# The offset convolution in 32 by 32 tiles with four bank exchanges, in place of two 64-wide column tiles

## The chip, the cores and the metric

The kernel runs on one core of a Trainium2 chip. The metric is the device time of one execution in microseconds (us); lower is better. TensorE is PE in the rows, its weight loads PEld; VectorE is DVE, ScalarE ACT, GpSimd POOL, SyncE SP.

## The reference, cut to what matters

Eight images of 32 channels and 192 by 192 pixels pass two layers, each with a group norm and a residual. The first layer has a 3 by 3 convolution that gives two offsets for every channel and pixel (`w_off`), bilinear sampling at these offsets, and a second 3 by 3 convolution of the samples. The change lies in the first of these convolutions.

```python
x = x + _L0_conv_ref(_gn(x), w_off, b_off, w_dcn, b_dcn)
x = x + _L1_conv_ref(_gn(x), w1, b1, w2, b2)
...
off = (jax.nn.sigmoid(conv2d(x, w_off, b_off, OFFSET * D, D)) - 0.5) * (2.0 * OFFSET)
...
v00 = planes[nidx, j0, i0]
...
sampled = v00 * (1 - wy) * (1 - wx) + v01 * (1 - wy) * wx + v10 * wy * (1 - wx) + v11 * wy * wx
return conv2d(sampled.reshape(b, c, h, w), w_dcn, b_dcn, P, D)
```

The second layer averages its normed input, makes a 3 by 3 kernel for each channel from the averages, and convolves each channel with it (depthwise).

## The kernel before, in words

The 128 partitions hold 32 channels of four neighbouring image rows (quarter g has row g of a group). A chunk is four such groups, 16 image rows; an image has 12 chunks, the program 96. All data are fp32, and TensorE runs an fp32 matmul in two passes, each with its own weight load, which stand as two records.

Each chunk has three views in `xv`: MID, its rows as they are, and ABOVE and BELOW, the same moved by one image row up and down. `xv` has three slots, filled by SyncE (`x_load`), with GpSimd setting the pads (`set_pads`).

The offset convolution is `offsets(n, i)`, at L402 through `conv`. For each offset i (across, down) and each half h of the chunk it makes six matmuls with 128 input rows, 64 output columns and 384 moving columns: the tap kx = 0, 1, 2, for two column tiles, the lower half of the partitions from ABOVE and the upper from BELOW. The weights `wos` are banded: a block of 128 by 64 holds the three vertical taps where they belong and zeros elsewhere. The result lies in the four PSUM banks of `z` (i, h). `off_mm` rises by one after i = 0 and by one after i = 1, and ScalarE's `offset(n, i)` (L614, Tanh of z into `du` or `dv`, signal `z_read`) waits for it; then come the signs `mu`, `mv` (L621), a mirrored row at an image's edge (L643) and the sizes (L628). VectorE selects neighbours by the signs (L818, L825, L826) and blends them (L835 to L851) into `sr`, shifted by SyncE into `sh`.

The program order on TensorE is written out by hand. In step i it does `depthwise(c, 0)`, `offsets(i, 0)`, `offsets(i, 1)`, `depthwise(c, 1)`, `deform(d, 0)`, `deform(d, 1)`, with c = i - 19 and d = i - 3. `deform` is the second convolution (`dc`, L442, and `fe` at an image's edge, L451), in four 32-wide column tiles of 128 rows. `depthwise` is the second layer's (`dw`, L475), in two 64-wide ones; `dw` is a single bank, and each depthwise half waits on `o_done` until ScalarE's `finish` (L649) has read the half before. ScalarE does, in step i: evacuation of dc (L669), sums for the next image (L655, L658), `finish(c, 0)`, Tanh, sign and size for i = 0 and for i = 1, `finish(c, 1)`, a square (L679), and `sides(i + 1)` (L635). The steps of an image's norm are small matmuls into `sm` and small GpSimd operations; `x_norm` in step 10 and `x_weights` in step 11 of an image make mean and scaled weights of the next (`wos` at L908).

Of the kernel before, what the change touches and what calls it, by code (L numbers as in the profile page):

```python
# [28 lines left out]
STILES = 8  # L29
SW = HW // G // STILES  # L30
# [36 lines left out]
def x_dmas(n):  # L67
    return 3 + (n % CHUNKS in (0, CHUNKS - 1))
# [37 lines left out]

def small_order():
# [13 lines left out]
def block_kernel(nc, x, planes, w_off, b_off, w_dcn, b_dcn, w1, b1, w2, b2, consts, xr, w_edge, pivots, w1x, out):  # L121
    with ExitStack() as ctx:
# [6 lines left out]
        xv = [sb(f"xv{s}", [P, 3, NB, WP]) for s in range(XS)]  # L129
# [14 lines left out]
        wo = sb("wo", [P, 2, 3, 2 * C])  # L144
        wo_sum = sb("wo_sum", [P, 2, 2 * C])
        wd_sum = sb("wd_sum", [P, Q, C])
        mr = [sb(f"mr{s}", [P, 1]) for s in range(2)]
        wos = [sb(f"wos{s}", [P, 2, 3, 2 * C]) for s in range(2)]
# [76 lines left out]
        off_mm = sem("off_mm")  # L225
        z_read = sem("z_read")
# [56 lines left out]
        def _(sp):  # L283
            def x_load(n):
# [4 lines left out]
                for view in range(3):  # L289
# [4 lines left out]
                    if j == CHUNKS - 1 and view == BELOW:  # L294
# [4 lines left out]
                                 blocks_of(b, line + P * k0, k1 - k0)).then_inc(done, 16)  # L299

# [94 lines left out]
        def _(pe):  # L395
# [3 lines left out]
            def conv(acc, weights, whole, moved):  # L399
                for kx in range(3):  # L400
                    for m, view in zip(halves, (whole, moved)):
                        last = nc.tensor.matmul(acc[m], weights[:, kx, :], view[:, :, kx:kx + W],  # L402
                                                start=kx == 0, stop=kx == 2)
                return last

            def offsets(n, i):
                b, j = divmod(n, CHUNKS)
                v = xv[n % XS]
                if i == 0:
                    pe.wait_ge(x_in[n % XS], ring(n, XS, x_dmas))  # L410
                    pe.wait_ge(pads, pads_set(n))
                    if j == 0:
                        pe.wait_ge(wo_ok, b + 1)
                wait(pe, z_read, 2 * (n - 1) + i + 1)
                for h in range(2):
                    k = slice(HALF * h, HALF * h + HALF)
                    last = conv(z[:, i, h, 0:HALF * W], wos[b % 2][:, i], v[:, ABOVE, k, :], v[:, BELOW, k, :])
                last.then_inc(off_mm, 1)
# [77 lines left out]
            def x_biases(b):  # L496
# [3 lines left out]
                for i in range(2):  # L500
                    for g, m in enumerate(quarters):
                        half = slice(C * (g % 2), C * (g % 2) + C)
                        nc.tensor.matmul(sm[m, C_OB + i:C_OB + i + 1], wo_sum[:, i, half], mean, start=True, stop=True)
# [50 lines left out]
            for i in range(TOTAL):  # L554
# [6 lines left out]
                offsets(i, 0)  # L561
                offsets(i, 1)
# [247 lines left out]
        def _(dve):  # L810
# [57 lines left out]
            dve.wait_ge(x_row, 1)  # L868
            for view in (ABOVE, BELOW):
# [287 lines left out]
```

## Time and profile before

| | before |
|---|---|
| median of 3 runs | 1492.13 us (1490.91 to 1494.03) |
| profiled execution, own time | 1493.54 us |
| its span, first to last instruction | 1491.7 us |
| mean granted TensorE clock | 0.992 of 2.4 GHz |
| busy: PE, DVE, ACT, POOL | 1436.3, 1257.4, 1152.9, 437.1 us |
| DMA | 308.77 MB, mean 207 GB/s |

Busy time is time in which an engine has at least one instruction in work. Matmuls overlap, so their mean duration (485 ns is common) is longer than the distance between their starts, and the distance is what one costs.

### The profile page before, as it was taken

The page shows a single profiled execution, that of the slowest core. Times are in us where ns is not written, and L with a number is a line of the kernel's source. Part 1 is how long each engine was busy: PE and PEld are TensorE (multiplying, and loading weights), DVE is VectorE, ACT ScalarE, POOL GpSimd, SP SyncE. Part 2 cuts the span into 40 slices and gives each one's busy share as a digit, 9 for nine tenths or more (in the row PEclk, how much of TensorE's full clock was granted, in tenths as well). Part 3 has the DMA queues.
Part 4 walks back from the last instruction along what each step waited for, and adds up shares of the span by engine and source line. Part 5 has one row for each costly group of instructions (what it writes and reads, how often), then busy time and mean ns, then how long its engine had stood idle before and what let it go on. Part 6 is the DMA issues. An engine that isn't in the chain of part 4 may idle for free.

```text
span 1491.7 us, 30369 instructions
## 1 busy us (share of the span) xinstructions
PE 1436.3 (96%) x12300; PEld 617.9 (41%) x12300; DVE 1257.4 (84%) x884; ACT 1152.9 (77%) x1970; POOL 437.1 (29%) x474
## 2 busy tenths in 40 slices
PE   5898798999999999999999999999999999999978
PEld 2333343444444444444444444444444444444433
DVE  4999999988888898889888988888888889888900
ACT  6789687986888778887888877888688877766643
POOL 5000734225050432306141151412505043230120
PEclk9999999999999999999999999999999999999999
DMA  8576587977888788886979778897888877767558
GB/s 270 159 191 170 146 215 182 242 197 204 236 224 217 198 213 228 228 216 179 244 206 255 189 206 230 223 233 194 205 236 224 217 199 180 198 179 201 140 145 260
DMA packets 226907, 308.77 MB, mean 207 GB/s; under 512 B 17216, under 2 KB 169152, under 8 KB 226768
## 3 DMA queue, kind: packets, MB, share of 16 engines
q1 hardware_dynamic: 211360, 266.68, 61.2%
q0 software_dynamic: 15408, 40.15, 17.3%
q8 instruction: 97, 1.59, 0.5%
q14 instruction: 42, 0.34, 0.1%
HBM read 190.35 MB, written 38.14 MB: 153 GB/s over the span
## 4 chain that ended last, share of the span: by engine, by line
PE 89%; DVE 4%; DMA 2%; issue 2%; ACT 2%; POOL 1%; SPq 0%; DVEq 0%; ACTq 0%; POOLq 0%
PE z L402 46%; PE dc L442 24%; PE dw L475 14%; PE z L475 3%; DMA yr<-in_planes 1%; DVE nb L840 1%; DVE nb L838 1%; DMA yh<-yr 1%; DVE nb L818 1%; DVE nb L835 0%; PE dc L451 0%; ACT nb L635 0%; DVE nb L844 0%; DVE nb L842 0%; PE z L494 0%
## 5 line engine op out<-in xcount | busy, mean ns | idle before, releaser
L402 PE MATMUL z<-xv,wos 128*64 128x384 f32 x4608 | 766.1, 488 | 10.7 <-issue 7.6
L402 PEld LDWEIGHTS z<-xv,wos 128*64 128x64 f32 x4608 | 330.7, 137 | 429.8 <-issue 428.6
L442 PE MATMUL dc<-sr,wds 128*32 128x384 f32 x2304 | 396.4, 489 | 13.4 <-issue 9.5
L442 PE MATMUL dc<-sh,wds 128*32 128x384 f32 x2304 | 396.4, 489 | 0.0
L1017 POOL DMA_DIRECT2D yr<-in_xr x96 | 86.2, 898 | 767.1 <-ACT yr L669 767.1
L818 DVE COPY_PREDICATED nb<-mu,xv 128x2280 f32<-128x2280 uint16 x96 | 269.2, 2804 | 36.9 <-ACT mu L621 36.5
L442 PEld LDWEIGHTS dc<-sr,wds 128*32 128x32 f32 x2304 | 133.5, 108 | 237.2 <-issue 237.1
L475 PE MATMUL dw<-yh,wy 128*64 128x388 f32 x616 | 229.7, 494 | 0.0
L475 PE MATMUL dw<-yr,wy 128*64 128x388 f32 x616 | 229.7, 494 | 0.0
L635 ACT ACTIVATE nb<-xv 128x2292 f32<-128x2292 f32 x96 | 202.9, 2113 | 28.8 <-DVE sr L851 20.6
L614 ACT ACTIVATE du<-z,ob 128x768 f32<-128x768 f32 x96 | 86.4, 900 | 128.8 <-PE z L402 128.2
L614 ACT ACTIVATE dv<-z,ob 128x768 f32<-128x768 f32 x96 | 86.4, 900 | 111.8 <-PE z L402 111.8
L825 DVE COPY_PREDICATED xv<-mv,xv 128x768 f32<-128x768 uint16 x96 | 102.6, 1069 | 83.0 <-ACT mv L621 61.0
L840 DVE TENSOR_TENSOR nb<-nb,xv 128x1536 f32<-128x1536 f32 x96 | 169.4, 1765 | 3.3
L835 DVE TENSOR_TENSOR nb<-nb,xv 128x1536 f32<-128x1536 f32 x96 | 169.2, 1763 | 3.3
L838 DVE TENSOR_TENSOR nb<-nb,du 128x1536 f32<-128x1536 f32 x96 | 169.0, 1761 | 3.3
L442 PEld LDWEIGHTS dc<-sh,wds 128*32 128x32 f32 x2304 | 132.2, 108 | 5.2 <-issue 5.0
L475 PEld LDWEIGHTS dw<-yr,wy 128*64 128x64 f32 x616 | 77.2, 135 | 111.3 <-issue 110.0
L669 ACT ACTIVATE yr<-dc,db 128x384 f32<-128x384 f32 x192 | 108.4, 571 | 5.7 <-PE dc L451 3.5
L851 DVE TENSOR_TENSOR sr<-nb 128x768 f32<-128x768 f32 x96 | 92.5, 963 | 12.9 <-DVE nb L844 0.5
L826 DVE COPY_PREDICATED nb<-mv,nb 128x768 f32<-128x768 uint16 x96 | 101.0, 1052 | 0.0
L679 ACT ACTIVATE junk<-yr,nmx 128x768 bf16<-128x768 f32 x96 | 88.7, 924 | 11.1 <-DMA yr<-in_xr 11.1
(130 smaller groups left out, 1594.6 us busy)
## 6 DMA issues: line engine op xcount, KB each, us to landing
xv<-in_x SPq DMA_DIRECT2D x272, 384.0 KB, 5.6
yr<-in_xr POOLq DMA_DIRECT2D x96, 392.0 KB, 5.0
out<-ot SPq DMA_DIRECT2D x96, 388.0 KB, 3.9
yh<-yr SPq DMA_DIRECT2D x178, 196.0 KB, 3.9
st<-in_planes SPq DMA_DIRECT2D x56, 576.0 KB, 7.5
sh<-sr SPq DMA_DIRECT2D x160, 194.0 KB, 5.1
sh<-sr SPq DMA_DIRECT2D x32, 145.5 KB, 5.7
yr<-in_planes SPq DMA_DIRECT2D x8, 576.0 KB, 10.3
```

The costliest lines, as they stand in the source:

```text
L402: last = nc.tensor.matmul(acc[m], weights[:, kx, :], view[:, :, kx:kx + W], start=kx == 0, stop=kx == 2)
L442: last = nc.tensor.matmul(dc[m, q, 0:NB * PAIRS], weights[:, kx, q], view[:, :, cols], start=first, stop=final)
L475: last = nc.tensor.matmul(acc[m], wy[b % 2][:, q, t], view[:, :, t:t + OW], start=t == 0, stop=t == 1)
L614: nc.scalar.activation(d[:].rearrange("p (h k) w -> p h (k w)", h=2), z[:, i, :, 0:HALF * W], ACT.Tanh, bias=ob[b % 2][:, i:i + 1], scale= ...
L635: nc.scalar.activation(nb[s][:, :, :, 1:W], v[:, :, :, 1:W], ACT.Copy)
L669: nc.scalar.activation(yr[:, k:k + NB, q, 1:PAIRS + 1], dc[:, q, 0:NB * PAIRS].rearrange("p (k w) -> p k w", w=PAIRS), ACT.Identity, bias= ...
L818: nc.vector.copy_predicated(q[:, :, :, 1:W - 1], m3[:, :, :, 1:W - 1], v[:, :, :, 3:W + 1]).then_inc(lerp, 1)
L825: nc.vector.copy_predicated(v[:, ABOVE, :, 1:W + 1], m1, v[:, BELOW, :, 1:W + 1]).then_inc(lerp, 1)
L826: nc.vector.copy_predicated(q[:, ABOVE], m1, q[:, BELOW]).then_inc(lerp, 1)
L835: nc.vector.tensor_tensor(two, two, own, ALU.subtract).then_inc(lerp, 1)
L838: nc.vector.tensor_tensor(two, two, u2, ALU.mult).then_inc(lerp, 1)
L840: nc.vector.tensor_tensor(two, two, own, ALU.add).then_inc(x_free, 1)
```

## The change

The offset convolution's matmuls become 32 by 32 tiles: one input row group g (a quarter of the partitions), one output row m, one tap (ky, kx). Each output row of a bank needs 9 such matmuls, 144 a chunk, and the array holds sixteen tiles. Two row groups may not write the same bank at once, so in phase p row group g works for bank (g + p) mod 4. Between phases TensorE waits for its own semaphore `z_turn`, which the last matmul of a phase raises. `tap_plan` decides which row group does which tap for which output row: three taps in phase 0, two in each of the phases 1 to 3. `off_mm` rises by two after the fourth phase; the wait for `z_read` stands before the first. To give each row group all the rows that it needs, a view has one slot more (`SLOTS`), filled by two small loads of 32 partitions, or by GpSimd or VectorE at an image's edge; pads are set for all 15 lines of `xv` in one operation. The weights are stored as nine dense 32 by 32 blocks for each i and row group: 576 elements a partition where there were 384.

```diff
 def x_dmas(n):
-    return 3 + (n % CHUNKS in (0, CHUNKS - 1))
+    return 5
...
+def tap_plan():
+    at = {ABOVE: 0, MID: SLOTS, BELOW: 2 * SLOTS}
+    plan = {}
+    for row in range(G):
+        source = {(g, g + view - row): at[view]
+                  for g in range(G) for view in (ABOVE, MID, BELOW) if 0 <= g + view - row <= 2}
+        if row == 0:
+            source[G - 1, 0] = at[MID] - 1
+        if row == G - 1:
+            source[0, 2] = at[MID] + 1
+        taps = sorted(itertools.product(range(3), range(3)), key=lambda t: sum(ky == t[0] for _, ky in source))
+        for bank in range(4):
+            room = [2 + (g == bank) for g in range(G)]
+            used = [[] for _ in range(G)]
...
+            plan[row, bank] = used
+    return plan
...
-        xv = [sb(f"xv{s}", [P, 3, NB, WP]) for s in range(XS)]
+        xs = [sb(f"xv{s}", [P, 3, SLOTS, WP]) for s in range(XS)]
+        xv = [t[:, :, 0:NB, :] for t in xs]
+        xf = [t[:].rearrange("p v k w -> p (v k) w") for t in xs]
...
-        wos = [sb(f"wos{s}", [P, 2, 3, 2 * C]) for s in range(2)]
+        wos = [sb(f"wos{s}", [P, 2, 9, C]) for s in range(2)]
...
+                if j > 0:
+                    sp.dma_start(xf[n % XS][P - C:P, SLOTS - 1, 1:W + 1],
+                                 lines[b, P * k - C:P * k, :]).then_inc(done, 16)
+                if j < CHUNKS - 1:
+                    sp.dma_start(xf[n % XS][0:C, SLOTS + NB, 1:W + 1],
+                                 lines[b, P * (k + NB):P * (k + NB) + C, :]).then_inc(done, 16)
...
-            def offsets(n, i):
+            def offsets(n, phase):
                 b, j = divmod(n, CHUNKS)
-                v = xv[n % XS]
-                if i == 0:
+                v = xf[n % XS]
+                if phase == 0:
                     pe.wait_ge(x_in[n % XS], ring(n, XS, x_dmas))
                     pe.wait_ge(pads, pads_set(n))
                     if j == 0:
                         pe.wait_ge(wo_ok, b + 1)
-                wait(pe, z_read, 2 * (n - 1) + i + 1)
-                for h in range(2):
-                    k = slice(HALF * h, HALF * h + HALF)
-                    last = conv(z[:, i, h, 0:HALF * W], wos[b % 2][:, i], v[:, ABOVE, k, :], v[:, BELOW, k, :])
-                last.then_inc(off_mm, 1)
+                    wait(pe, z_read, 2 * n)
+                else:
+                    pe.wait_ge(z_turn, 3 * n + phase)
+                for t in range(3 if phase == 0 else 2):
+                    for g, rows in enumerate(quarters):
+                        bank = (g + phase) % 4
+                        i, h = divmod(bank, 2)
+                        for m in range(G):
+                            at, ky, kx = plan[m, bank][g][t]
+                            last = nc.tensor.matmul(z[quarters[m], i, h, 0:HALF * W],
+                                                    wos[b % 2][rows, i, 3 * ky + kx],
+                                                    v[rows, at + HALF * h:at + HALF * h + HALF, kx:kx + W],
+                                                    start=phase == 0 and t == 0, stop=phase == 3 and t == 1)
+                if phase < 3:
+                    last.then_inc(z_turn, 1)
+                else:
+                    last.then_inc(off_mm, 2)
...
-                offsets(i, 0)
-                offsets(i, 1)
+                for phase in range(4):
+                    offsets(i, phase)
...
+                    ts(xf[n % XS][r, at, 1:W + 1], zero[r, 0:W], m[r], None, ALU.add).then_inc(x_row, 1)
...
-                for view in (ABOVE, BELOW):
-                    last = ts(v[:, view, :, 0:WP:WP - 1],
-                              zero[:, 0:2 * NB].rearrange("p (k e) -> p k e", e=2), m[:], None, ALU.add)
-                last.then_inc(pads, 1)
+                ts(xf[n % XS][:, 0:3 * SLOTS, 0:WP:WP - 1], zero[:, 0:6 * SLOTS].rearrange("p (k e) -> p k e", e=2),
+                   m[:], None, ALU.add).then_inc(pads, 1)
```

The order on TensorE in step 19, the first with a depthwise part, from `depthwise(c, 0)` to the start of `deform`, before (matmuls as the program has them, two records each; the waits in brackets):

```order
L475 MATMUL dw<-yr,wy 64x388 [waits y_sh0,wy_ok]
L475 MATMUL dw<-yh,wy 64x388
L475 MATMUL dw<-yr,wy 64x388
L475 MATMUL dw<-yh,wy 64x388
L402 MATMUL z<-xv,wos 64x384 [waits z_read,pads,x_in1]
L402 MATMUL z<-xv,wos 64x384 x11
L402 MATMUL z<-xv,wos 64x384 [waits z_read]
L402 MATMUL z<-xv,wos 64x384 x11
L475 MATMUL dw<-yr,wy 64x388 [waits o_done]
```

And the same place now:

```order
L528 MATMUL dw<-yh,wy 64x388
L464 MATMUL z<-xv,wos 32x384 [waits z_read,pads,x_in1]
L464 MATMUL z<-xv,wos 32x384 x47
L464 MATMUL z<-xv,wos 32x384 [waits z_turn]
L464 MATMUL z<-xv,wos 32x384 x31
L464 MATMUL z<-xv,wos 32x384 [waits z_turn]
L464 MATMUL z<-xv,wos 32x384 x31
L464 MATMUL z<-xv,wos 32x384 [waits z_turn]
L464 MATMUL z<-xv,wos 32x384 x31
L528 MATMUL dw<-yr,wy 64x388 [waits o_done]
```

24 matmuls with one wait in their middle have become 144 with three, each on the matmuls just before it.

The order on GpSimd at an image's boundary (the end of step 10 and step 11), before:

```order
L930 TENSOR_SCALAR xv<-zero,mx 32x192 [waits x_free,x_step,off_mm]
L1017 DMA yr<-in_xr 128x784 [waits x_row,y_done]
L930 TENSOR_SCALAR xv<-zero,mx 32x192 [waits x_free,off_mm]
L936 TENSOR_SCALAR xv<-zero,mx 128x4x2 [waits x_row]
L936 TENSOR_SCALAR xv<-zero,mx 128x4x2
L903 TENSOR_TENSOR mr<-nmx,rx 128x1
L904 TENSOR_TENSOR rxs<-kc,rx 128x1
L908 TENSOR_SCALAR wos<-wo,rx 128x384 [waits off_mm]
```

And now:

```order
L986 TENSOR_SCALAR xv<-zero,mx 32x192 [waits x_free,x_step,off_mm]
L987 TENSOR_SCALAR xv<-zero,mx 32x192
L1072 DMA yr<-in_xr 128x784 [waits x_row,y_done]
L986 TENSOR_SCALAR xv<-zero,mx 32x192 [waits x_free,off_mm]
L987 TENSOR_SCALAR xv<-zero,mx 32x192
L992 TENSOR_SCALAR xv<-zero,mx 128x15x2 [waits x_row]
L957 TENSOR_TENSOR mr<-nmx,rx 128x1
L958 TENSOR_TENSOR rxs<-kc,rx 128x1
L962 TENSOR_SCALAR wos<-wo,rx 128x576 [waits off_mm]
```

Each edge row has a second beside it, two pad operations have become one, and the operation on `wos` has grown.

## Rows read from the trace of the kernel before

**Rows 1.** The page: busy time of the engines, and the last chain by line

```profile
PE 1436.3 (96%) x12300; PEld 617.9 (41%) x12300; DVE 1257.4 (84%) x884; ACT 1152.9 (77%) x1970; POOL 437.1 (29%) x474
...
PE z L402 46%; PE dc L442 24%; PE dw L475 14%; PE z L475 3%; DMA yr<-in_planes 1%; DVE nb L840 1%; DVE nb L838 1%; DMA yh<-yr 1%; DVE nb L818 1%; DVE nb L835 0%; PE dc L451 0%; ACT nb L635 0%; DVE nb L844 0%; DVE nb L842 0%; PE z L494 0%
```

**Rows 2.** The last chain in order of time: start us, us, what

```profile
119.68 7.89 PE z L402 x48
...
133.06 7.89 PE z L402 x48
...
291.70 7.74 PE z L402 x48
306.25 7.74 PE z L402 x48
```

**Rows 3.** Windows: us, then busy us of PE, PEld, DVE, ACT, POOL

```profile
645.90:823.00 177.10, 177.10 (x1538) 75.99 (x1536) 156.01 (x109) 144.74 (x249) 52.69 (x56) 1.00 0.83 217
```

**Rows 4.** Timeline around 713.3 us: start us, us, engine line op, tile, form

```profile
712.90 0.49 PE L475 MATMUL dw<-yh,wy 128*64 128x388 f32 x1
...
713.32 0.52 PE L442 MATMUL dc<-sr,wds 128*32 128x384 f32 x2
...
713.33 0.52 PE L442 MATMUL dc<-sh,wds 128*32 128x384 f32 x2
...
713.67 0.49 PE L442 MATMUL dc<-sr,wds 128*32 128x384 f32 x2
713.67 0.12 PEld L442 LDWEIGHTS dc<-sr,wds 128*32 128x32 f32 x2 [0.19 <-issue]
```

**Rows 5.** Timeline from 506.9 to 511.7 us, TensorE

```profile
506.90 0.52 PE L442 MATMUL dc<-sr,wds 128*32 128x384 f32 x2
...
510.94 0.54 PE L475 MATMUL dw<-yr,wy 128*64 128x388 f32 x1
...
511.32 0.49 PE L475 MATMUL dw<-yr,wy 128*64 128x388 f32 x1
...
511.65 0.49 PE L475 MATMUL dw<-yr,wy 128*64 128x388 f32 x1
```

**Rows 6.** Timeline: a chunk's last z records, ScalarE after them, and a burst of small matmuls

```profile
504.85 0.81 PE L402 MATMUL z<-xv,wos 128*64 128x384 f32 x4
...
505.71 0.90 ACT L614 ACTIVATE dv<-z,ob 128x768 f32<-128x768 f32 x1 [1.35 <-PE z L402]
...
508.13 0.57 ACT L649 ACTIVATE ot<-dw,wb 128x388 f32<-128x388 f32 x1
...
1451.38 0.71 PE L530 MATMUL sm<-hid,w2r 128*32 128x2 f32 x64
...
261.33 0.17 PE L530 MATMUL sm<-hid,w2r 128*32 128x2 f32 x1
```

**Rows 7.** Timeline: the last chunk on ScalarE and VectorE, and TensorE's wait after it

```profile
1405.60 0.90 ACT L614 ACTIVATE dv<-z,ob 128x768 f32<-128x768 f32 x1 [1.36 <-PE z L402]
...
1407.86 1.07 DVE L825 COPY_PREDICATED xv<-mv,xv 128x768 f32<-128x768 uint16 x1 [1.44 <-ACT mv L643]
...
1425.57 0.52 PE L442 MATMUL dc<-sr,wds 128*32 128x384 f32 x2 [2.50 <-issue]
```

**Rows 8.** Timeline: GpSimd at the boundary of two images, and the next image's first z

```profile
514.21 1.34 POOL L930 TENSOR_SCALAR xv<-zero,mx 32x192 f32<-32x192 f32 x1
...
518.28 3.81 POOL L908 TENSOR_SCALAR wos<-wo,rx 128x384 f32<-128x384 f32 x1
...
527.10 0.81 PE L402 MATMUL z<-xv,wos 128*64 128x384 f32 x4
```

**Rows 9.** Timeline: the edge products of dc (fe) between two halves, TensorE

```profile
389.90 0.49 PE L442 MATMUL dc<-sr,wds 128*32 128x384 f32 x1
...
390.41 0.52 PE L442 MATMUL dc<-sr,wds 128*32 128x384 f32 x2
390.47 0.43 PE L451 MATMUL dc<-fe,wde 128*32 128x96 f32 x6
```

More of the change, by code:

```diff
@@ L1 @@
+import itertools
 from contextlib import ExitStack
@@ L104, in split_cols, with place @@
     return slice(at, at + PAIRS)
+def tap_plan():
[12 more added lines that the diff above has]
+            used = [[] for _ in range(G)]
+            def place(i):
+                if i == len(taps):
+                    return True
+                ky, kx = taps[i]
+                for g in sorted(range(G), key=lambda g: sum(a == g for a, _ in source)):
+                    if (g, ky) in source and len(used[g]) < room[g]:
+                        used[g].append((source[g, ky], ky, kx))
+                        if place(i + 1):
+                            return True
+                        used[g].pop()
+                return False
+            assert place(0)
+            plan[row, bank] = used
+    return plan
 def small_order():
@@ L397, in _ @@
             quarters = [slice(C * g, C * g + C) for g in range(G)]
[L399 to L404, printed above, removed]
-            def offsets(n, i):
+            plan = tap_plan()
+            def offsets(n, phase):
                 b, j = divmod(n, CHUNKS)
-                v = xv[n % XS]
-                if i == 0:
+                v = xf[n % XS]
+                if phase == 0:
                     pe.wait_ge(x_in[n % XS], ring(n, XS, x_dmas))
@@ L500, in x_biases @@
                 for i in range(2):
-                    for g, m in enumerate(quarters):
-                        half = slice(C * (g % 2), C * (g % 2) + C)
-                        nc.tensor.matmul(sm[m, C_OB + i:C_OB + i + 1], wo_sum[:, i, half], mean, start=True, stop=True)
+                    for m in quarters:
+                        for ky in range(3):
+                            nc.tensor.matmul(sm[m, C_OB + i:C_OB + i + 1], wo_sum[0:C, i, ky], mean[0:C],
+                                             start=ky == 0, stop=ky == 2)
                 for q in range(Q):
@@ L867, in _ @@
                 .then_inc(x_row, 1)
[L868 to L873 removed]
+            nc.vector.tensor_scalar(xf[0][P - C:P, SLOTS - 1, 1:W + 1], zero[P - C:P, 0:W], m[P - C:P], None,
+                                    ALU.add).then_inc(x_row, 1)
+            dve.wait_ge(x_row, 2)
+            nc.vector.tensor_scalar(xf[0][:, 0:3 * SLOTS, 0:WP:WP - 1],
+                                    zero[:, 0:6 * SLOTS].rearrange("p (k e) -> p k e", e=2), m[:], None,
+                                    ALU.add).then_inc(pads, 1)
             dve.wait_ge(loaded, LOADED)
@@ L934, in set_pads @@
                     return
-                for view in (ABOVE, BELOW):
-                    last = ts(v[:, view, :, 0:WP:WP - 1],
-                              zero[:, 0:2 * NB].rearrange("p (k e) -> p k e", e=2), m[:], None, ALU.add)
-                last.then_inc(pads, 1)
+                ts(xf[n % XS][:, 0:3 * SLOTS, 0:WP:WP - 1], zero[:, 0:6 * SLOTS].rearrange("p (k e) -> p k e", e=2),
+                   m[:], None, ALU.add).then_inc(pads, 1)
             def set_s_pads(n):
```

23 lines of the change are left out of this document (13 added, 10 removed).

## The prediction

> **What bounds the kernel now.** The page comes first: TensorE is busy 96% of the span, VectorE 84%, ScalarE 77%; in the chain that ended last the offset convolution (z, L402) has 46% and the other two convolutions (dc L442, dw and z L475) 41% [rows 1]. A share is an average, so next the stages. In the chain in order of time the reader should compare distances between the starts of z. Before the depthwise products join (chunks 0 to 18) they lie 13.4 us apart, though z (7.89) and dc (4.0, from 506.90 to 510.94) need only 12 [rows 2, 5]: another engine sets the pace. From chunk 19 on they lie 14.55 us apart and z takes 7.74 us of it [rows 2]. A whole image of that stage takes 177.1 us, TensorE busy throughout, VectorE 156.01 us, 13.0 a chunk, which makes it the engine that paced the early chunks [rows 3]. So a shorter z block is worth its full size in 77 chunks (19 to 95), until a chunk reaches VectorE's pace, 13.0 to 13.4 us; in the first 19 it is worth nothing.
>
> **The unit of work.** z holds 48 matmul records in 7.74 us: each fp32 matmul is two passes, two column tiles run side by side, so 24 pass times of 0.3225 us. In the 32-wide tiles of dc four start at 713.32 and 713.33, side by side, and after the first, longer pass they step at the same rate: 12 pass times in the 3.9 us from 506.9 to 510.9 [rows 4, 5]. So a pass costs 0.3225 us however many tiles share it, and the new block needs 9 matmuls per tile, 18 passes: 5.81 us in place of 7.74, 1.93 us less.
>
> **What is added to that**, all per chunk.
> Changing the tile shape. From dw to dc the step between starts is 0.42 us where it is 0.33 within dw: 0.095 more, and the first pass is 0.025 longer (713.32 to 713.67). After a change into dw the first step is 0.38 for 0.33 [rows 4, 5]. Today z has dw's shape and changes at neither end. The new block pays at both: 0.095 + 0.095 + 0.05 = 0.24 us, and 4 x 0.025 = 0.10 us for the first passes of its phases.
> The three turns. A phase starts when the last matmul of the one before is complete. The last z pass starts at 505.17 (four records from 504.85, the last ends 0.49 after its start) and ScalarE, waiting for it, starts at 505.71: 0.54 us [rows 6]. TensorE behind its own semaphore I take like that, at 0.55 us start to start, where streaming has 0.3225: 0.23 x 3 = 0.69 us.
> The ramp of a phase. Its end is that of the sixteenth tile, so the stagger of starts counts four times. Four dc tiles start within 0.02 us after a change of shape, 0.007 us a tile [rows 4]: 15 x 0.007 = 0.10 us, 0.41 us a chunk. This supposes that the instructions behind a wait are queued already. The bound from above is a long burst of small ones: 64 passes in 0.71 us, one record of them 0.17, start over 0.54 us, 0.0086 us a pass, 0.0172 a matmul [rows 6], so 0.26 us a ramp. I take 0.10, because a phase, too, starts after a pause. The bound from below is none of it, and turns at no cost.
> The block is then 5.81 + 0.24 + 0.10 + 0.69 + 0.41 = 7.25 us: 0.49 us less than 7.74.
>
> The Trainium skill ("TensorE: Matmul & The Clock Gate", Measured speedup vs the span model) gives about 4 ns per extra tile. By it a ramp would be 0.06 us and the chunk 0.16 us shorter still; no row here has sixteen tiles.
>
> A new wait. off_mm now rises by two at the end of the fourth phase, so ScalarE's first Tanh loses the half block that it had as a lead: now it idles 1.35 us more between the two [rows 6]. After it, all follows the end E of the block: 0.05 for the release, dv, mv and size 2.42 (505.71 to 508.13), du, mu and size the same, finish 0.57: 5.46 us after E, 5.5 with TensorE's release, where finish now ends 3.04 after [rows 6]. TensorE's next dw(c+1,0) needs that bank. It now starts at 510.94, E + 5.28 [rows 5]; the change of shape in front makes that 5.4. So 0.1 us is waited on `o_done` in each chunk, with the whole PE queue behind it. Net gain per chunk 0.39 us, 30 us over 77.
> ScalarE then has to run through its chunk after E: an image holds 144.74 us of its work, 12.1 a chunk against 14.2 [rows 3], so it keeps up. VectorE starts later by up to 3.9 us, but deform(i-3) asks for nothing later than samples of chunk i-2, and VectorE works on i-1 by then, 13 us a chunk: that hides it.
>
> Where nothing hides it: head and tail. In the last chunk VectorE's L825 stands idle 1.44 us before the mirrored mv comes. du's Tanh, with which VectorE's chunk begins, moves from the half block to its end, 3.9 us later against E; less the idle 1.44, L825 comes 2.4 us later, and mv, now behind one block of 2.42, as much. dc waits 2.50 us for what follows already, so the end moves by the same 2.4 us [rows 7]. Chunk 0 has the same chain and loses that less the 0.5 us gained on its block: 1.9. Together 4 us.
>
> GpSimd at an image boundary. It sets pads and scales wos for the next image: 3.81 us for 384 elements, ending 522.09; the next image's z starts 5.0 us later, at 527.10 [rows 8]. The chain begins with ScalarE's evacuation, 2.4 us later against TensorE; there is one more 32x192 row (1.34), and wos has 576 elements (3.81 x 1.5, 1.9 more): 5.6 us, over the 5.0. I take 0.9 us in each of six images, 5 us; nothing and 12 us are the ends.
> The two added loads (32 partitions each) go out right behind the chunk's own loads, for a chunk that is used two steps later: nothing. One pads instruction for two, and two column groups of x_biases against one: nothing.
>
> **The sum.** 1493.54 (the profiled execution, 1.41 above the median of the three timed) - 30 + 4 + 5 = 1472.5; against the median that is 1471.
>
> **Rivals.**
> *Overheads at their upper ends (slower).* One mechanism: sixteen tiles cannot be started at 0.007 us each, since queued instructions run out and the sequencer feeds one pass per 0.0086 us. Four ramps of 0.26 instead of 0.10 add 0.64 us a chunk, 49 us: 1520. It decides from 0.17 us a ramp on: 21 us of gain over 77 chunks is 0.27, or 0.07 a ramp. For it: the 64-pass burst; against: starts 0.007 apart after a pause.
> *Row groups don't run side by side (the change doesn't do what it says; slower).* If passes queue by column group in program order, a second pass waits for the first and the next row group stands behind it: each matmul adds one pass time. Phases of 13, 9, 9, 9 passes give 12.9 us, with overheads 14.3, 6.6 more than 7.74: 77 x 6.7 + 19 x 5 for the early chunks, 1492 + 611 = about 2100. For it: in the fe products, sr of the next half starts 0.19 us after its columns came free (389.90 + 0.32), so an instruction does stand behind another tile's queue. Against: it starts before the last six fe passes do [rows 9]; every row here spans all 128 rows, so the trace can't say whether queues belong to columns or to tiles.
> *Weight loads no longer hidden.* Today the load of the next pass starts in the same 0.01 us as the running pass, and is 0.12 us long, all hidden [rows 4]. If not: 18 x 0.11 = 2.0 us a chunk, 77 x 2.0 = 152, and about 3 in the early chunks: 1629. The Trainium skill (same page, "What overlaps and what doesn't") says that LDWEIGHTS overlaps a running MATMUL only when the row group differs. By that rule this is the outcome; the row shows loads beside passes of the same 128 rows, so it disagrees.
> *Turns cheaper, or tiles start at once (faster).* Without the 0.69 and 0.41 the chunk would be 13.1, under VectorE's pace: 77 x 1.3 = 100 less 9 gives 1401. Half of it: 1435. For it: matmul ends in the records are modelled, and no row shows a wait of TensorE for itself. Against: the Tanh does start 0.54 us after the last pass.
>
> **How the numbers follow.** Forecast (1455 to 1489) 0.42; overheads high (1489 to 1530) 0.23; cheaper turns (1400 to 1455) 0.18; row groups in line 0.11; loads exposed 0.06. The range 1425 to 1530 takes in the first two and most of the third, some 0.8; the forecast's own is 1455 to 1489. What a measurement tells from no change is 0.2%, 3 us. Faster: 0.42 + 0.18 and a small part of the second, 0.63; same 0.06; slower 0.31.
>
> **What would show it.** z's matmul records 288 a chunk, in four groups of 16 tiles; passes 0.32 us apart; starts within a round over 0.1 us; 0.55 us from a phase's last start to the next phase; z block 7.25 us; du waiting once per chunk on z with dv following at once; idle before dw on ACT ot of 0.15 us; distance of z 14.2 us. Passes of one column in line would show the second rival, PEld before each pass the third. A ScalarE that no longer waits for z at all would make it wrong too.

## The result, and the profile after

| | before | after |
|---|---|---|
| median of the timed runs | 1492.15 us | 1677.13 us (1673.78 to 1684.41) |
| profiled execution: own time, span | 1493.54, 1491.7 us | 1684.41, 1682.6 us |
| distance of z blocks, undisturbed | 14.55 us | 15.73 us |
| undisturbed z block | 7.74 us | 8.64 us |

A block or chunk is called undisturbed when no wait or stop falls into it. The ratio is 1.1245, 95% interval 1.1205 to 1.1285: 12% slower, where 1.4% faster was forecast, and outside the range. The page of the changed kernel (busy time, last chain by line, instruction queue) beside [rows 1]:

```profile
PE 1568.5 (93%) x35596; PEld 666.2 (40%) x35596; DVE 1272.2 (76%) x884; ACT 1142.6 (68%) x1970; POOL 364.9 (22%) x466
...
PE z L464 51%; PE dc L495 20%; PE dw L528 13%; PE z L528 3%; ACT du L668 1%; ACT du L682 1%; ACT dv L668 1%; ACT dv L682 1%; DMA yr<-in_planes 1%; ACT junk L733 0%; DVE st L912 0%; PE sm L556 0%; ACT ot L703 0%; PE dc L504 0%; DMA yr<-in_xr 0%
...
q8 instruction: 279, 4.57, 1.2%
```

TensorE executes three times as many records, and its instruction queue moves 279 packets of 16 KB; before there were 97:

```profile
q8 instruction: 97, 1.59, 0.5%
```

The chain in order of time, one undisturbed chunk of after, to set beside [rows 2]:

```profile
936.60 1.52 PE dw L528 x8
938.12 2.71 PE z L464 x94
940.88 1.94 PE z L464 x63
942.86 1.94 PE z L464 x63
944.84 1.92 PE z L464 x63
946.76 1.45 PE dw L528 x8
948.22 4.05 PE dc L495 x47
952.33 1.52 PE dw L528 x8
953.85 2.71 PE z L464 x94
```

The four phases can be read off: 2.71 us, then three of 1.94, with 0.04 of idle time at each turn, 8.64 us from 938.12 to 946.76. The chunk is 15.73 us: 1.18 more than before, 0.90 of it in z. One image of this stage (window columns as in [rows 3]) is 200.2 us, where it was 177.1; 12 x 15.73 explains only 188.8 of them, and TensorE is idle for 6.0 of the 200.2:

```profile
604.80:805.00 200.20, 194.18 (x4461) 81.94 (x4458) 157.95 (x108) 143.41 (x248) 45.56 (x56) 0.99 0.77 197
```

What TensorE waited for, from the table of waits (us in total, times, longest):

```profile
PE z L464 <- issue: 27.0, 23, 6.6
PE sm L538 <- ACT ys L753: 19.0, 8, 5.3
...
PE z L464 <- ACT dv L668: 10.6, 3, 3.6
PE dc L495 <- issue: 7.1, 4, 3.9
PE sm L584 <- issue: 3.9, 2, 3.6
PE dw L528 <- ACT ot L703: 3.3, 7, 0.7
```

"issue" is time without a releaser that the profile shows. Before, L485 (now L538) waited 5.6 us in two places, and z's `issue` was one wait of 7.6, at 167 us. So there are three losses to explain: the undisturbed z block (predicted 7.25, is 8.64), waits on ScalarE, and stops of TensorE that name nobody.

**Inside a phase.** The second phase of another chunk, TensorE's matmul records in short windows (in brackets the passes that run in it):

```profile
701.70:702.10 0.40, 0.34 (x18) 1.00 1.08 300
702.10:702.40 0.30, 0.30 (x32) 1.00 0.87 251
702.40:702.64 0.24, 0.24 (x18) 1.00 0.20 52
702.64:702.80 0.16, 0.16 (x23) 1.00 0.00 0
```

and the timeline of moments within it (the first passes of the first round and its second passes; then two single weight loads):

```profile
701.79 0.62 PE L464 MATMUL z<-xv,wos 32*32 32x384 f32 x16
...
702.14 0.80 PE L464 MATMUL z<-xv,wos 32*32 32x384 f32 x16
...
702.46 0.10 PEld L464 LDWEIGHTS z<-xv,wos 32*32 32x32 f32 x1 [0.22 <-issue]
...
702.65 0.10 PEld L464 LDWEIGHTS z<-xv,wos 32*32 32x32 f32 x1
```

Sixteen first passes start between 701.79 and 701.90 (the last ends at 702.41, 0.51 long), their second passes from 702.14 on: as predicted, 0.007 us a tile and all sixteen side by side. The second round's first tile goes on in time, at 702.46. Then nothing starts for 0.19 us: the next weights are loaded at 702.65, 0.03 us after the very first matmul's second pass has ended (702.14 + 0.48 = 702.62), and from there one matmul begins every 0.017 us, not every 0.007. The phase's last pass starts at 703.23, 1.44 us behind its first; four passes a tile, 0.3225 us apart, and the ramp of 0.11 would put it at 1.1. **Theory A:** an fp32 matmul is four records (two weight loads, two passes); TensorE's queue holds about sixteen matmuls until they have finished, so with sixteen tiles the next round isn't in the queue when its tiles come free, and enters it only as the first round leaves. The Trainium skill ("TensorE: Matmul & The Clock Gate", the table ahead of its first section) gives the queue's depth as 64 with a partial reorder window; sixteen matmuls of four records are just that. No row counts the places of the queue. An estimate from the rows alone (each matmul waits for the end of the seventeenth before it, as the eighteenth does here for the first; 0.017 us between entries, 0.3225 us a pass) gives 1.42 us from the first to the last start of this phase, where the trace has 1.44.

### The profile page after: what moved, and what is told of

Same layout as the page of the kernel before. It is cut to its first block, busy times and chain, and to the rows that moved or that the text cites. A ratio compares the mean times of both kernels' runs of the same rounds, so it can differ in the third digit from the quotient of the medians.

```text
span 1682.6 us, 77129 instructions
## 1 busy us (share of the span) xinstructions
PE 1568.5 (93%) x35596; PEld 666.2 (40%) x35596; DVE 1272.2 (76%) x884; ACT 1142.6 (68%) x1970; POOL 364.9 (22%) x466
## 2 busy tenths in 40 slices
DMA packets 235554, 316.19 MB, mean 188 GB/s; under 512 B 20032, under 2 KB 177600, under 8 KB 235232
## 4 chain that ended last, share of the span: by engine, by line
PE 88%; issue 5%; ACT 5%; DMA 1%; DVE 0%; POOL 0%; SPq 0%; ACTq 0%; DVEq 0%; POOLq 0%
PE z L464 51%; PE dc L495 20%; PE dw L528 13%; PE z L528 3%; ACT du L668 1%; ACT du L682 1%; ACT dv L668 1%; ACT dv L682 1%; DMA yr<-in_planes 1%; ACT junk L733 0%; DVE st L912 0%; PE sm L556 0%; ACT ot L703 0%; PE dc L504 0%; DMA yr<-in_xr 0%
## 5 line engine op out<-in xcount | busy, mean ns | idle before, releaser
L464 PE MATMUL z<-xv,wos 32*32 32x384 f32 x27648 | 860.4, 499 | 56.8 <-issue 27.0
L464 PEld LDWEIGHTS z<-xv,wos 32*32 32x32 f32 x27648 | 377.8, 103 | 528.1 <-PE z L464 223.0
L872 DVE COPY_PREDICATED nb<-mu,xv 128x2280 f32<-128x2280 uint16 x96 | 274.7, 2862 | 287.9 <-ACT mu L675 287.9
L495 PE MATMUL dc<-sr,wds 128*32 128x384 f32 x2304 | 400.8, 493 | 5.7 <-issue 5.7
L495 PE MATMUL dc<-sh,wds 128*32 128x384 f32 x2304 | 401.1, 493 | 1.4 <-issue 1.4
L528 PE MATMUL dw<-yr,wy 128*64 128x388 f32 x616 | 236.4, 505 | 5.2 <-ACT ot L703 3.3
L528 PE MATMUL dw<-yh,wy 128*64 128x388 f32 x616 | 237.9, 507 | 0.1
L528 PEld LDWEIGHTS dw<-yr,wy 128*64 128x64 f32 x616 | 71.6, 136 | 138.2 <-issue 136.4
L905 DVE TENSOR_TENSOR sr<-nb 128x768 f32<-128x768 f32 x96 | 102.3, 1066 | 12.8 <-DVE nb L898 0.5
L898 DVE TENSOR_TENSOR nb<-nb,dv 128x768 f32<-128x768 f32 x96 | 93.5, 974 | 3.3
```

The source lines that it names most:

```text
L464: last = nc.tensor.matmul(z[quarters[m], i, h, 0:HALF * W], wos[b % 2][rows, i, 3 * ky + kx], v[rows, at + HALF * h:at + HALF * h + HALF, ...
L495: last = nc.tensor.matmul(dc[m, q, 0:NB * PAIRS], weights[:, kx, q], view[:, :, cols], start=first, stop=final)
L528: last = nc.tensor.matmul(acc[m], wy[b % 2][:, q, t], view[:, :, t:t + OW], start=t == 0, stop=t == 1)
L872: nc.vector.copy_predicated(q[:, :, :, 1:W - 1], m3[:, :, :, 1:W - 1], v[:, :, :, 3:W + 1]).then_inc(lerp, 1)
L905: nc.vector.tensor_tensor(by_parity, side, own, ALU.add).then_inc(sampled, 1)
```

## The experiments

**1. One phase.** The four phases made one; each row group stays at one bank for nine rounds (leaves out what the other row groups add to that bank).

```diff
-                for t in range(3 if phase == 0 else 2):
+                for t in range(9):
...
-                for phase in range(4):
-                    offsets(i, phase)
+                offsets(i, 0)
...
```

> The changed kernel with its four phases made one: each row group stays at one bank and does nine rounds of its own taps, so the sums of the other row groups are left out and the output is not the reference's; the sixteen tiles, their shapes and their 144 matmuls a chunk stay, the three waits of TensorE on itself go. Theory A (window): TensorE's queue holds about 64 records, that is 16 or 17 fp32 matmuls of four records, and a place comes free only when the oldest has ended, so the matmul after the seventeenth is late in every round: z block near 7.7 us a chunk, total near 1600 us. Rival B (restart): the late seventeenth matmul is a cost of starting again behind a wait, some 0.35 us once a phase: one phase pays it once, block near 6.4 us, total near 1500 us. Rival C (neither; the prediction's own arithmetic): 6.0 us.

Measured: 1643.69 us, ratio 1.1007 (1.0988 to 1.1025). The chain shows an undisturbed block of

```profile
945.86 7.76 PE z L464 x280
```

So without a turn nine rounds still cost as much as the old block: A's 7.7, not the 6.4 or 6.0. A turn costs (8.64 - 7.76) / 3 = 0.29 us, net of what it spares: with turns, fewer rounds are late. The time as a whole was 44 us above what A expected: the unnamed stops doubled (55.6 us in 51 places).

**2 and 3. Eight and twelve tiles.** Four phases, but only row groups 0 and 1 (72 matmuls a chunk), or all but row group 3 (108); leaves out the taps of the others. One execution each.

```diff
-                    for g, rows in enumerate(quarters):
+                    for g, rows in enumerate(quarters[:2]):
```

> The changed kernel with row groups 2 and 3 left out: eight tiles in place of sixteen, 72 matmuls a chunk, the same four phases and waits; the taps of the two groups are left out of the sums. Theory A (window of 16 or 17 matmuls): two rounds fit the window, so nothing is late: undisturbed z block near 6.8 us, phases 2 to 4 step 1.04 us from first to last start. Rival B (restart behind a wait): the late start comes at the same time after a wait as now (0.86 us), so phases stay near 1.44 us and the block near 8.4. Both expect passes of 0.32 us.

> The changed kernel with row group 3 left out: twelve tiles, 108 matmuls a chunk, the same phases; that group's taps are left out of the sums. Theory A (window of 16 or 17): the sixth matmul of the second round waits for the first one's end: phases 2 to 4 take about 1.30 us from first to last start, block near 8.0 us. Without a window, or if only sixteen tiles at once slowed each other: 1.07 us and 6.95.

The z blocks in the chain, first with twelve tiles (1602.35 us), then with eight (1530.99 us):

```profile
939.90 2.51 PE z L465 x72
942.45 1.80 PE z L465 x48
944.30 1.80 PE z L465 x48
946.15 1.79 PE z L465 x48
947.93 1.45 PE dw L530 x8
```

```profile
938.67 2.18 PE z L465 x48
940.90 1.60 PE z L465 x32
942.54 1.60 PE z L465 x32
944.19 1.52 PE z L465 x32
945.71 1.45 PE dw L530 x8
```

8.03 us with twelve (A near 8.0, without a window 6.95) and 7.04 with eight (A 6.8). The pass count per tile is the same in all three; with the number of tiles the block grows by 1.0 and 0.6 us. That fits a limit on matmuls in flight and not a price of turns or shapes. Eight is 0.24 us over what A gives, which stays unexplained; 8.4, what a restart after each wait would give, it is not.

**4. Late release alone.** The kernel before; ScalarE is told once, at the end of the z block.

```diff
-                wait(pe, z_read, 2 * (n - 1) + i + 1)
+                if i == 0:
+                    wait(pe, z_read, 2 * n)
...
-                last.then_inc(off_mm, 1)
+                if i == 1:
+                    last.then_inc(off_mm, 2)
```

> The kernel before with one edit: off_mm rises by two after the whole block and the wait for z_read stands before the first half alone, so ScalarE has both Tanhs behind the block's end as in the change. The prediction's step: 4 us at head and tail, and TensorE's next dw at E + 5.28 against a release at E + 5.5, 0.2 us in 77 chunks: 15 us; together 19, near 1511 us. Rival: the lead is slack and costs nothing but the head and tail: 1496 us.

Measured: 1536.8 us, ratio 1.0296 (1.0277 to 1.0314): +44, more than twice what was expected. Its waits:

```profile
PE sm L487 <- ACT ys L701: 20.0, 8, 5.2
...
PE dw L477 <- ACT ot L651: 14.3, 46, 0.7
```

An undisturbed chunk is 14.83 us, 0.29 more. And in each image TensorE waits 1.98 us for the sums of y, a wait that nobody had costed: ScalarE makes these sums at the end of its chunk, and TensorE asks for them at the end of its own. Where the clock falls after that wait (three of six images) the chunk is 18.47 us long from dw to dw, else 16.77, where it was 14.93. Per image: 12 x 0.29 + 1.6 to 3.3 = 5.1 to 6.8; seven such images and a bit are the 44.

**5. Turns alone.** The kernel before with three waits of TensorE on itself in each z block.

```diff
+                if i == 1:
+                    pe.wait_ge(off_mm, 2 * n + 1)
...
+                    if h == 1:
+                        last.then_inc(z_turn, 1)
+                        pe.wait_ge(z_turn, 2 * n + i + 1)
```

> The kernel before with three waits of TensorE on its own last matmul in each z block, one before every quarter of it, nothing else changed: the price of a turn by itself, with two tiles at work. From start to start a turn takes 0.54 us in the trace of the changed kernel against 0.32 of streaming, and the next first pass is 0.025 longer: 0.24 each, 0.73 a chunk, z block 8.47 us, 77 chunks 56 us: near 1548 us. If a wait also emptied the queue and made what follows late (rival B), by 0.2 us or more a turn beyond that: 1595 us or more.

Measured: 1571.99 us, ratio 1.0544 (1.0517 to 1.057).

```profile
940.05 1.96 PE z L403 x12
942.06 2.18 PE z L403 x12
944.37 2.17 PE z L403 x12
946.59 2.16 PE z L403 x12
948.74 1.30 PE dw L481 x8
```

The block is 8.69 us, 0.95 more: 0.32 a turn (expected 0.24). Times 77 chunks this is 73 of the 81 us. In the first 19 chunks, which another engine paces, the same longer block costs 4.5 us in all (257.3 us from the first z to that of chunk 19, for 252.8). The price of a turn was sized a little low, in the same sense as experiment 1 shows it (0.29).

**6. More records alone.** The kernel before, each z matmul cut into four of 96 columns.

```diff
-                    for m, view in zip(halves, (whole, moved)):
+                    for part in range(4):
+                        for m, view in zip(halves, (whole, moved)):
...
```

> The kernel before with each z matmul cut into four of 96 columns: the same products in the same two column tiles, no further waits, but 96 z matmuls a chunk where there were 24, so TensorE's records per chunk go from 224 to 512 (the changed kernel: some 700). Theory: beside the window the changed kernel pays stalls of 1 to 2 us at irregular places, in which TensorE waits for nothing that the profile shows, because its instruction stream is longer (instruction queue packets 279 in place of 97). By it such stalls appear here, some 0.3 to 0.6 us a chunk on average, instruction packets near 200, z block itself 7.9 us, total near 1540 us. Rival: the stalls belong to the sixteen tiles or the turns: none here, total near 1506 us.

Measured: 1517.9 us, ratio 1.0172 (1.015 to 1.0193); block 7.97 us. Instructions more than doubled (27,648 more records), and stops hardly appeared, which seemed to clear the instruction stream. It didn't, as the next runs show; two stops, of 0.85 and 2.46 us, were there, each ending 1.30 us behind a packet of the kind told of next.

**What the stops end with.** The longest stop inside z in the timeline, the window of it, and the instruction queue's row for 908.3 to 909.4 us:

```profile
910.78 0.57 PE L464 MATMUL z<-xv,wos 32*32 32x384 f32 x10 [1.64 <-issue]
```

```profile
909.20:910.70 1.50, 0.00 (x0) 0.00 (x0) 0.00 (x0) 0.00 (x0) 0.00 (x0) 1.00 1.15 246
```

```profile
q8 instruction: 1, 0.02, 5.3%
```

TensorE's last pass ends at 909.14. A 16 KB packet of the instruction queue runs from 908.40 to 909.34, and 1.44 us behind its end TensorE goes on, while the 16 DMA engines are busy throughout. All 17 unnamed stops over 0.25 us between 400 and 1500 us (16.8 us together) end 1.25 to 1.55 us behind such a packet. **Theory F:** they are late instruction fetches. A packet brings 256 records (71,192 records over 279 packets). From the records that TensorE had begun when each fetch started, less 256 for each fetch before it, the earliest fetches start at some 150 to 160 and the latest at 449: about 300 records of slack. In z the kernel before goes through them at 12 a us, the changed one at 67: 4.5 us, in which the fetch has to get its turn among the data packets. The Trainium skill ("Advanced Engine Details and Errata", ISA Cache) gives lines of 16 KB, 256 instructions, which the trace agrees with. For how many there are it has both "Only 2 cache lines!" and "32KB (128KB on TensorE)"; the 300 records of slack here are far less than the 2048 that 128 KB would hold, an estimate from that section's 256 instructions in 16 KB.

**7. Lighter DMA.** The changed kernel; leaves out three quarters of each load of xv after the third chunk and of each store, so 206.78 MB are moved, not 316.19.

```diff
+                    if n >= XS:
+                        k1 = k0 + 1
...
-                sp.dma_start(out[b, :, NB * j:NB * j + NB], ot[n % 2][:])
+                sp.dma_start(out[b, :, NB * j:NB * j + 1], ot[n % 2][:, 0:1])
```

> Leaves out three quarters of each load of xv after the first three chunks, and three quarters of each store of the output, so that about 105 of the 316 MB are not moved; TensorE, ScalarE, VectorE and GpSimd do the same instructions. Theory F (the irregular stops of TensorE are late instruction fetches: in the changed kernel 17 of the stops over 0.25 us between 400 and 1500 us that have no named releaser end 1.3 to 1.55 us behind the end of a 16 KB packet of the instruction queue, and TensorE consumes one such packet of 256 records in 3.8 us of a z block; the fetch waits its turn behind the data packets): with a third of the data gone most stops go, the mean z block falls from 9.07 to under 8.8 us with a median that stays 8.64, the mean chunk distance (chunks 36 to 84) from 16.8 to about 16.2, and the time from 1677 to about 1645 us. Rival (the stops are made by the sixteen tiles or the turns inside TensorE, whatever the DMA queues carry): block mean and time stay within 0.5% of the changed kernel, 1670 to 1685.

Measured: 1651.22 us, ratio 1.107 (1.1052 to 1.1089), mean block 8.88 us with the median at 8.63, chunk distance 16.43. F, in size too, though the block and the chunk fell less than it said. Not a single TensorE instruction was changed, and 26 us went. Its waits have

```profile
PE z L466 <- issue: 16.3, 17, 7.5
```

and the unnamed stops over 0.25 us that end 1.2 to 1.6 us behind a packet, 27 of 27.7 us in the changed kernel, are 16 of 9.3 us here. That names 18 of the 26 us; what else a lighter traffic does was not separated.

**8. Eight parts.** As 6, but 48 columns.

> The kernel before with each z matmul cut into eight of 48 columns: no 32 by 32 tiles, no turns, four tiles never more than two side by side, but 768 instruction records of TensorE in a z block. With the +0.23 us that the cut into four cost for 72 more matmuls, the undisturbed block is about 8.3 us, that is 93 records a us, against 67 a us in the changed kernel (0.43 us of stops in a mean block), 74 in the kernel of one phase (0.85) and 54 and 48 in the kernels of twelve tiles and of the cut into four (nearly none). Theory F (late instruction fetches, which come in when TensorE takes over about 60 records a us): stops that end 1.3 to 1.6 us behind a packet of the instruction queue in most blocks, at least 1.2 us of them a chunk, and 1620 to 1750 us. Rival (stops belong to sixteen tiles or turns): no stops, about 1545 us.

Measured: 2069.37 us, one execution. The stops of F are there, 174.1 us in 116 places, without one 32 by 32 tile; 106 of the 121 unnamed stops over 0.25 us end 1.2 to 1.6 us behind a packet, a stretch that by chance would catch 7%. So the rival falls. The time is far above F's range for another reason, and the undisturbed block of 8.3 us was wrong:

```profile
939.73 6.16 PE z L405 x210
945.89 0.89 issue
946.77 3.94 PE z L405 x127
```

210 passes in 6.16 us are 0.029 us each, 384 of them 11.3 us, where half of what a pass of 96 columns costs (192 in 7.97 us) is 0.021. That makes 68 records a us, not 93. By rows of the waits (z on issue) the stops line up with how fast and how long records are used up:

| kernel | records a us in z | records in a block | z waited on issue: us, times |
|---|---|---|---|
| before | 12 | 96 | 7.6, 1 |
| 6, four parts | 48 | 384 | 7.8, 3 |
| 3, twelve tiles | 54 | 432 | 9.8, 4 |
| after | 67 | 576 | 27.0, 23 |
| 1, one phase | 74 | 576 | 55.6, 51 |
| 8, eight parts | 68 | 768 | 174.1, 116 |

Each but the last holds one of 6.6 to 8.0 us, between 167 and 188 us into the run, which ends behind no packet. At one length of block (576) the faster kernel has more stops, and at nearly one speed (67 and 68) the one with longer blocks.

**9. The averaging matmuls a chunk later.**

```diff
+                if b and o == 4:
+                    y_means(b - 1)
                 for phase in range(4):
...
-                if b and o == 3:
-                    y_means(b - 1)
```

> The changed kernel with the matmuls that average the sums of y (line L538) moved from the end of a chunk's work to behind the first dw matmuls of the next chunk. In the changed kernel TensorE waits 1.82 us for them in each of seven images, and the chunk with the wait is 3 to 5 us longer than the one beside it, against 0.9 before. If this wait comes from ScalarE's later start (theory L: the release of both halves at the block's end), the move takes 1.8 us and what follows it (the clock) away in each of seven images: 1655 us, 1650 to 1665. Rival (the wait only moves on, to the next z block, which waits for ScalarE as well): 1672 to 1680.

Measured: 1668.28 us (1663.2 to 1681.7), ratio 1.1195 (1.1144 to 1.1245). The wait is gone and 9 us with it, less than half of what was expected and at the edge of what the interval can tell; the chunk that had it is 16.2 us where no stop falls into it, for 17.66. The stops vary from run to run and hide the rest; neither the forecast of 1650 to 1665 nor the rival's 1672 to 1680 was met. What follows the wait was not the same each time either: two windows of after, each right behind a wait of 1.82 us, and one behind a stop of 3.62 us (the column behind the engines is the granted clock):

```profile
461.30:465.00 3.70, 3.70 (x48) 1.29 (x49) 3.63 (x3) 3.70 (x7) 0.26 (x1) 0.54 0.40 107
```

```profile
862.40:866.00 3.60, 3.60 (x98) 1.93 (x112) 3.53 (x3) 3.60 (x7) 0.18 (x1) 1.00 0.50 145
```

```profile
896.30:900.00 3.70, 3.70 (x44) 1.54 (x43) 3.63 (x3) 1.40 (x4) 0.00 (x0) 0.50 0.86 235
```

1.00 is 2.4 GHz, 0.50 the lower level of 1.2 GHz. After the first and third wait the next passes take twice as long, after the second they don't: the same pause costs 1.8 us or 1.8 and the fall.

**10. Turns and late release together.** 4 and 5 in one kernel.

> The kernel before with both: TensorE's three waits on itself (alone +81 us) and both halves released at the end of the block (alone +44 us). If the two add, 1617 us. If the late release costs less once the z block is longer, because ScalarE then finishes the dw output before TensorE comes to its second dw matmuls (the wait of 0.22 us a chunk, 22 of the 44 us, goes), 1592 to 1600. That is the case of the changed kernel, where this wait stands in one chunk of twelve alone.

Measured: 1607.69 us, one execution, between the two. The undisturbed chunk is 15.70 us with a z block of 8.60, and TensorE still waits 0.23 us in it for ScalarE's ot. So the expectation had the mechanism wrong: the wait does not shrink with a longer z block, since ScalarE starts only at its end. It was for the first dw block of the next chunk, not the second. In the changed kernel the same holds, only the idle time is nearly covered by the longer dw and dc. Call it theory L: ScalarE's chain behind the late release paces this part of the chunk.

```profile
931.07 0.90 ACT L668 ACTIVATE du<-z,ob 128x768 f32<-128x768 f32 x1 [3.32 <-PE z L464]
...
935.88 0.57 ACT L703 ACTIVATE ot<-dw,wb 128x388 f32<-128x388 f32 x1
```

Seven instructions of ScalarE, 5.38 us from 931.07 to 936.45, and dw 0.15 behind them, at 936.60 (in the chain of after).

**11. ScalarE's copy earlier.** The changed kernel:

```diff
-                size(i, 1)
                 if c >= 0:
                     finish(c, 1)
+                size(i, 1)
```

> The changed kernel with one instruction of ScalarE moved: the copy of the second dw output (ot, line L703) stands ahead of the last Abs on dv, not behind it. In the changed kernel each dw block ahead of a z block starts 0.12 to 0.15 us after this copy ends, and the time from the end of a z block to that start is at least 5.56 us in undisturbed chunks (0.04 to ScalarE's start, 5.38 of ScalarE's seven instructions, 0.14), against 5.31 in the kernel before, where the copy had been done 2.25 us. Theory L (ScalarE's chain behind the late release paces this part): the copy ends 0.83 us earlier, TensorE's own work of about 5.35 us is the bound, the undisturbed chunk falls from 15.73 to 15.50 to 15.60 us and the time by 10 to 18 us, from 1677 to about 1663. Rival (this part is longer because TensorE's own dw and dc blocks are, by the changes of tile shape): 15.73 and no change of the time. Where VectorE is the bound, in the first chunks, the later Abs could cost a little.

Measured: 1664.18 us (1660.18 to 1667.17), ratio 1.1171 (1.1153 to 1.119); undisturbed chunk 15.59 us. Theory L, in both numbers (0.14 us in 77 chunks is 11): 13 us hung on one copy's place in ScalarE's queue.

**12. All three together.** 7, 9 and 11 in one kernel (leaves out what 7 does).

> The changed kernel with the three edits of the runs before at once: light loads and stores (leaves out three quarters of each load of xv after the first three chunks and of each store), the averaging matmuls of y a chunk later, ScalarE's copy earlier. What is left of the loss is then the z block alone (8.64 against 7.74 us) with the changes of tile shape, and what remains of late fetches (3 us an image in the run with light loads). By the account: undisturbed chunk 15.55, an image 177.1 + 12 x 1.0 + 3 = 192 against 201.8 in the changed kernel (mean of images 4 to 8) and 197.1 with light loads alone; time 1610 to 1630 us. If the three overlap (they take away the same idle time), 1640 to 1650.

Measured: 1619.11 us, ratio 1.0865 (1.0844 to 1.0885); an image 193.3 us. The three give 58 us, by themselves 26 + 9 + 13 = 48: they don't overlap. The 10 us more are near what single runs of the changed kernel differ by (1673.78 to 1684.41). Part of them the granted clock can show: in the 72 chunks from 19 on it was at 0.50 for 20.5 us in the changed kernel, 10.2 in experiment 7 and never here. Over these chunks TensorE stood idle for 46.5 us in the changed kernel (window 310.90 to 1523.50 us) and for 19.5 here (292.40 to 1454.10); the kernel before, not at all.

No kernel here beats the one before, and no experiment points to one that would.

## Why the prediction was wrong

**The step that failed** is "So a pass costs 0.3225 us however many tiles share it, and the new block needs 9 matmuls per tile, 18 passes: 5.81 us". Each pass does take 0.3225 and sixteen do run side by side, but the next round can't start at once. By the prediction's own terms a block without turns is 5.81 + 0.24 + 0.02 + 0.10 = 6.2 us; experiment 1 measured 7.76. That 1.6 us turns the 1.93 us of gain into nearly nothing (7.76 for 7.74), and the turns make it a loss. In the changed kernel, with five late rounds in place of eight, the block is 8.64 for 7.25, 1.4 more than forecast: over 77 chunks 107 of the 206 us between the forecast 1471 and the measured 1677. That the next round can't start is measured; that a full queue is why is theory A, which four kernels fit, and which no run that changed the records of a matmul has tested. Rows of four tiles of one row group can't show it: four tiles have four rounds in a queue of sixteen matmuls. One row hinted at it, and was read as a price per start only: in the burst of 64 passes [rows 6] the starts are regular until 1451.64, where the 17th matmul loads its weights, 0.03 us behind the end of the first, and irregular from there on. Its price it couldn't show, since the mean step is 0.0086 us on either side. Taken as "0.0086 us a pass, only in the ramp" it became the rival with overheads at their upper end, at 0.64 us a chunk in place of 1.6. Its mechanism (queued instructions run out) was near the truth, its size and place were not: the ramps are short, the rounds behind them late.

**What was right.** Sixteen tiles side by side, against the rival of 2100 us; weight loads hidden, against the one of 1629; the ramp: 0.11 us for 0.10; a turn 0.54 us start to start for 0.55. All in all a turn costs 0.29 to 0.32 us, for 0.23 plus a ramp of 0.10. VectorE's lateness is mostly hidden: no wait of dc on it is named, and the unnamed one in the last chunk grew from 2.50 to 3.85 us, where 2.4 us more were expected.

**The late release** was sized in its place and missed in another. For the start of the next dw the prediction had E + 5.5 us, where the trace has 5.57, and 11 confirms what it is worth (0.14 us a chunk). Missing was the wait for the sums of y, once an image, with the fall of the clock that can follow. Head and tail: the first Tanh starts 7 us later (35.6 for 28.4), and behind the last z pass the end comes 0.9 us later (87.5 for 86.6), where 1.9 and 2.4 were expected. GpSimd at the image boundary cost nothing, where 5 us were taken: the 576 elements of wos take 1.73 us, not the 5.7 scaled up from [rows 8], and TensorE waits for GpSimd nowhere there.

**The instruction stream** was no term of the sum, and no reason was given for that. Stops behind its packets are 27.7 us in the changed kernel, and experiment 7 took 18.4 of them away with 26 us of time.

**Two slips of the sum**, too small to matter: the rival with exposed loads adds up to 1626 (1471 + 152 + 3), not 1629, and 5.6 over 5.0 is 0.6 us at an image's boundary, where 0.9 was taken.

**The account**, from the starts of the z blocks in the two profiled executions, whose spans lie 191 us apart. 34 us fall before chunk 19 (286.4 us from the first z to that of chunk 19, for 252.8), 150 in the 72 chunks after (16.84 us each for 14.76), 7 behind them. The 150 are: z block 0.90 x 72 = 65; the dw and dc blocks beside other tile shapes (15.59 - 14.55 - 0.90) x 72 = 10; ScalarE's copy 0.14 x 72 = 10; waits for the averaging matmuls 11; the stops over 0.25 us that name nobody 17; waits for ot once an image 3; and 20.5 us at the lower clock, which cost half of that, 10, by an estimate from the passes that took twice as long. That is 126, and 24 were not separated. In experiment 12 these chunks lose 99, again the 65, the 10 and 24. Of the 34 us before chunk 19, experiment 12 takes 18 away. Little of them can be the z block, since experiment 5 made it 0.95 longer and lost 4.5 there; the 15 that stay are open.

## What to carry to other kernels

Tiles side by side paid here only as far as the next round could start in time. If theory A is right, with fp32 matmuls of four records it is tiles times four that must be counted against TensorE's queue; read a burst of small matmuls in a trace of before to see where its starts become irregular. Count also records a us: when a matmul gets smaller, the same work is used up in more instructions, and their fetches share the DMA engines with the data; a stop without a releaser that ends at a fixed distance behind a packet of the instruction queue is that. When a release moves to the end of a block, go through everything that the released engine does last in its chunk, what is done once an image too, not only the first wait on it.

## What the runs showed of the hardware

- Matmuls in flight: a round of sixteen fp32 tiles, 0.645 us at two passes of 0.3225, takes 7.76 / 9 = 0.86 us on average over nine rounds. That the limit is a count of records was argued from 8, 12 and 16 tiles and from the moment of the late weight load; no run varied the records per matmul.
- Instruction fetches of 16 KB for 256 records, about 300 records of slack, and 1.25 to 1.55 us from the end of a late one to the next matmul (17 stops of the changed kernel; 106 of 121 in experiment 8 lie within 1.2 to 1.6).
- 48-column passes on two tiles cost 0.029 us each; those of 96 columns added 0.23 us to a block of 7.74.
- Of two waits of 1.82 us of TensorE, one was followed by the lower clock and the other not; what decides it stays open.
